# Marks up to sixteen ahead of each wait in a pair of tiles, and GpSimd's low parts after the counting

## What is computed

```python
xn = layernorm(x)
# graph part, twice: h = xn @ W.T + b; agg = segment_sum(h[src], dst); relu
# mixing part: q = softmax(xn @ Wq.T) * 512**-0.5; k = softmax(xn @ Wk.T, over nodes); v = xn @ Wv.T
#   y = q @ (k.T @ v) + xn;  y @ W1.T @ W2.T + y
x = x + graph + mixing
x = x + moe(layernorm(x))       # 8 experts, gates by 8 Sinkhorn rounds, top 156 rows each
```

## Time and profile before

| | us |
|---|---|
| median of 3 executions | 470.5 (470.48, 470.50, 472.29) |
| profiled execution, its own time | 470.02 |
| its span | 468.1 |
| PE busy in the span | 449.9 |
| DVE busy in the span | 333.2 |
| POOL busy in the span | 66.1 |

### The profile page before, as it was taken

How to read it: one execution, slowest core, us unless ns; L and a number is a source line. 1 busy time by engine, 2 the same in 40 slices (tenths; PEclk the granted TensorE clock), 3 DMA queues, 4 the chain that set the end, 5 groups by cost and what they waited for, 6 DMA issues and landing times.

```text
span 468.1 us, 7042 instructions
## 1 busy us (share of the span) xinstructions
PE 449.9 (96%) x2517; PEld 362.0 (77%) x2517; DVE 333.2 (71%) x1116; ACT 150.3 (32%) x274; POOL 66.1 (14%) x95
## 2 busy tenths in 40 slices
PE   8999999999999999899998999999999999888996
PEld 5877788889797979788787999877777775655783
DVE  5988599867868686888879960344545667777982
ACT  3666784223132323322240100223033124551120
POOL 5424700000000000000012000001400000006662
PEclk9999999999999999999999999999999999999999
DMA  8920200540000000203000000001844449405891
GB/s 250 265 78 2 90 0 1 137 97 11 1 1 0 2 1 8 85 0 127 1 5 2 2 0 1 1 0 20 296 131 133 133 135 366 170 1 169 295 366 73
DMA packets 20414, 40.46 MB, mean 86 GB/s; under 512 B 2521, under 2 KB 2851, under 8 KB 20373
## 3 DMA queue, kind: packets, MB, share of 16 engines
q1 hardware_dynamic: 18117, 32.53, 22.7%
q0 software_dynamic: 2256, 7.39, 4.5%
HBM read 30.09 MB, written 10.31 MB: 86 GB/s over the span
## 4 chain that ended last, share of the span: by engine, by line
PE 78%; DVE 13%; ACT 4%; issue 2%; DMA 1%; POOLq 0%; DVEq 0%; POOL 0%; SPq 0%
PE ps L769 29%; PE ps L1132 9%; PE ps L1024 9%; PE ps L952 6%; PE ps L897 6%; PE ps L756 4%; PE ps L970 2%; PE ps L811 2%; DVE RING_S L1877 2%; DVE RING_D L1876 2%; ACT scrap_a L1557 1%; DVE QTL L1811 1%; PE ps L1149 1%; ACT QTH L1287 1%; PE ps L945 1%
## 5 line engine op out<-in xcount | busy, mean ns | idle before, releaser
L1876 DVE TENSOR_SCALAR RING_D<-places,PLACES 125x170 bf16<-125x170 f16 x274 | 71.0, 259 | 3.2 <-issue 3.2
L1877 DVE TENSOR_SCALAR RING_S<-iota,HOME 125x128 bf16<-125x128 f16 x274 | 68.1, 249 | 0.0
L1024 PE MATMUL ps<-AT,H1H 125*128 125x416 f32 (+1 forms) x120 | 42.9, 358 | 0.3 <-ACT AT L1452 0.3
L1024 PE MATMUL ps<-AT,H1L 125*128 125x416 f32 (+1 forms) x120 | 42.2, 351 | 0.0
L756 PE MATMUL ps<-RING_D,RING_S 125*125 125x170 bf16 x274 | 35.2, 244 | 2.5 <-DVE RING_S L1877 0.9
L756 PEld LDWEIGHTS ps<-RING_D,RING_S 125*125 125x125 bf16 x274 | 27.5, 136 | 13.1 <-DVE RING_S L1877 7.1
L1132 PE MATMUL ps<-H2H,AT 125*125 125x512 f32 x90 | 36.1, 402 | 0.0
L1132 PE MATMUL ps<-H2L,AT 125*125 125x512 f32 x90 | 35.5, 394 | 0.0
L1149 PE MATMUL ps<-WE0H 128*128 128x512 f32 x129 | 35.5, 408 | 0.0
L630 POOL TENSOR_TENSOR G2L<-RAW_G,G2H 128x512 fp32r<-128x512 f32 x4 | 5.0, 1286 | 184.9 <-ACT G2H L1287 184.9
L1947 DVE TENSOR_TENSOR ps<-ps,bias 125x512 f32<-125x512 f32 x20 | 14.0, 699 | 20.4 <-PE ps L769 20.4
(11 more groups left out here) (413 smaller groups left out, 1156.5 us busy)
## 6 DMA issues: line engine op xcount, KB each, us to landing
RAW_E<-in_experts SPq DMA_DIRECT2D x8, 1024.0 KB, 9.9
RAW_AGAIN<-in_experts SPq DMA_DIRECT2D x3, 1024.0 KB, 9.5
X<-in_x SPq DMA_DIRECT2D x1, 2240.0 KB
out_x<-X SPq DMA_DIRECT2D x10, 224.0 KB
scratch<-X SPq DMA_DIRECT2D x10, 224.0 KB
scratch<-Y SPq DMA_DIRECT2D x10, 224.0 KB
RAW<-in_mW2T SPq DMA_DIRECT2D x4, 256.0 KB, 4.3
RAW_A<-in_mW SPq DMA_DIRECT2D x4, 256.0 KB, 4.7
```

The costliest lines, as they stand in the source:

```text
L1024: mm = pe.matmul(PS[plan[f"z{ch}_{f}"][0]][:, 0:c1 - c0], h[0:TT, k, 128 * f:128 * (f + 1)], AT[0:TT, k, c0:c1], start=(k == 0 and n == 0) ...
L1876: V.tensor_scalar(hot_d(v, width(b)), places[0:ET, 0:width(b)], PLACES[0:ET, c:c + 1], None, ALU.is_equal)
L1877: V.tensor_scalar(hot_s(v), iota[0:ET, :], HOME[0:ET, c:c + 1], None, ALU.is_equal).then_inc(done["marked"], 1)
```

## The change

The visits are laid a little differently: three instead of two at each of six places of the context, one fewer in `attend` of pairs 0 to 3 and in the second mix of pairs 1 to 3, one more in h2. In a pair DVE's steps get a new order. The eight matmuls with the identity of one `attend` become four of twice the columns, ahead of the wait for qtl_ready. Tile 9 is turned in the middle of the last mix of pair 3 (into another PSUM bank), and its low part stands ahead of that pair's last sum. Five marks go from behind the branch to ahead of it. POOL makes G2L only after all counts are stored.

```diff
--- before.py
+++ after.py
@@ -134,7 +134,7 @@
         for i in (2 * p, 2 * p + 1):
             use(f"xq{i}", (2, 3), ("mix_added", i + 1))
             if i + 2 < NT:
-                use(f"qt{i + 2}", (7,), ("qth_ready", i + 3), ("qtl_ready", i + 3))
+                use(f"qt{i + 2}", (7 if i + 2 < NT - 1 else 6,), ("qth_ready", i + 3), ("qtl_ready", i + 3))
     for i in range(NT):
         use(f"h{i}", (6, 7, 0, 1), ("h1h_ready", i + 1), ("h1l_ready", i + 1))
     for ch in range(3):
@@ -199,14 +199,14 @@
 def visits_in_products():
 
 
-    spots = [("cp", n, 2) for n in range(12, 48, 6)]
+    spots = [("cp", n, 3) for n in range(12, 48, 6)]
     for p in range(PAIRS):
         a, b = 2 * p + 2, 2 * p + 3
         if a < NT:
             spots += [(f"q{a}", 6, 7 if p else 5)]
-        spots += [(f"a{p}", 28, 8)]
+        spots += [(f"a{p}", 28, 7 if b < NT else 8)]
         if b < NT:
-            spots += [(f"q{b}", 6, 7), (f"x{a - 2}", 6, 7), (f"x{b - 2}", 6, 8)]
+            spots += [(f"q{b}", 6, 7), (f"x{a - 2}", 6, 7), (f"x{b - 2}", 6, 7 if p else 8)]
         else:
             spots += [(f"x{a - 2}", 0, 4), (f"x{a - 2}", 6, 5), (f"x{b - 2}", 6, 9)]
     for i in range(NT - 1):
@@ -666,6 +666,7 @@
                     link(ins)
             ins.then_inc(done["ranges"], 1)
 
+            pool.wait_ge(done["adj_hi"], NG)
             for c in range(C):
                 split_lo("g2", c)
 
@@ -937,12 +938,14 @@
                 for h in range(2):
                     ps = opens(f"at{p}_{h}")
                     visits(f"a{p}", 28 * h)
+                    both = ps[:, 0:4 * (TT + 1)].rearrange("p (k t n) -> p k t n", k=2, t=2)
+                    for n, x in enumerate((XTL, XTH)):
+                        pe.matmul(both, identr[:], x[:, 2 * p:2 * p + 2, 2 * h:2 * h + 2, 0:TT + 1].rearrange("p t k n -> p k t n"),
+                                  start=(n == 0), stop=False, skip_group_check=True)
                     for k in range(2):
                         f = 2 * h + k
                         block = slice(128 * f, 128 * (f + 1))
                         o = ps[:, 2 * (TT + 1) * k:2 * (TT + 1) * (k + 1)]
-                        for n, x in enumerate((XTH, XTL)):
-                            pe.matmul(o, identr[:], x[:, 2 * p:2 * p + 2, f, 0:TT + 1], start=(n == 0), stop=False, skip_group_check=True)
                         if f == 0:
                             pe.wait_ge(done["qtl_ready"], 2 * p + 2)
                             if p == 0:
@@ -952,11 +955,11 @@
                                 mm = pe.matmul(o, w[:, c, block], q[:, c].rearrange("p t n -> p (t n)"), start=False, stop=(c == C - 1 and n == 2), skip_group_check=True)
                     closes(f"at{p}_{h}", mm)
 
-            def mix(i):
+            def mix(i, **kw):
 
                 p, t = i // 2, i % 2
                 product(f"xq{i}", opens(f"xq{i}")[0:TT, :], (lambda c: SH[:, c, t, 0:TT], lambda c: SL[:, c, t, 0:TT]), (rows_of(MPH), rows_of(MPL)),
-                        before=lambda c: pe.wait_ge(done["sl_ready"], 2 * p + c // 2 + 1), unit=f"x{i}")
+                        before=lambda c: pe.wait_ge(done["sl_ready"], 2 * p + c // 2 + 1), unit=f"x{i}", **kw)
 
             pe.wait_ge(*lo_of("wv", C - 1))
             n = 0
@@ -980,9 +983,12 @@
                 if b < NT:
                     tile_product(f"q{b}", b, WQH, WQL, unit=f"q{b}")
                 for i in (2 * p, 2 * p + 1):
-                    mix(i)
-                    if i + 2 < NT:
-                        turn_q(i + 2)
+                    if i + 2 == NT - 1:
+                        mix(i, between=lambda: turn_q(NT - 1), at=7)
+                    else:
+                        mix(i)
+                        if i + 2 < NT:
+                            turn_q(i + 2)
             pe.wait_ge(*lo_of("g1", C - 1))
             for i in range(NT):
                 tile_product(f"h{i}", i, G1H, G1L, unit=f"h{i}")
@@ -1479,8 +1485,10 @@
                 if b < NT:
                     scale_q(b)
                     round_q(a)
+                if b == NT - 1:
+                    round_q(b)
                 groups_ending(f"x{b - 2}")
-                if b < NT:
+                if b < NT - 1:
                     round_q(b)
                 if b == NT - 1:
                     for c in range(C):
@@ -1907,39 +1915,43 @@
             context_left(3)
             for p in range(PAIRS):
                 a, b = 2 * p + 2, 2 * p + 3
-                mark_next(5)
+                mark_to(f"a{p}")
                 if a < NT:
                     q_peak(a)
+                    mark_next(3)
+                    q_inverse(a)
+                    mark_to(f"q{b}")
+                    attn_left(p, 0)
+                    mark_to(f"x{a - 2}")
+                    mark_next(2)
+                    attn_left(p, 1)
+                    mark_to(f"x{b - 2}")
+                    q_peak(b)
+                    mark_next(3)
+                    q_inverse(b)
+                    mark_to(f"q{a + 2}" if a + 2 < NT else f"a{p + 1}")
+                    add_mix(a - 2)
+                    q_left(a)
+                    if b < NT - 1:
+                        mark_next(3)
+                        add_mix(b - 2)
+                        q_left(b)
+                    else:
+                        q_left(b)
+                        mark_next(3)
+                        add_mix(b - 2)
                 else:
                     split_lo("g1", 0)
                     split_lo("g1", 1)
-                mark_to(f"a{p}")
-                if a < NT:
-                    q_inverse(a)
-                mark_next(3)
-                attn_left(p, 0)
-                if b < NT:
-                    mark_to(f"q{b}")
-                else:
+                    mark_to(f"x{a - 2}")
+                    attn_left(p, 0)
                     split_lo("g1", 2)
+                    attn_left(p, 1)
                     split_lo("g1", 3)
-                attn_left(p, 1)
-                if b < NT:
-                    mark_next(4)
-                    q_peak(b)
-                mark_to(f"x{a - 2}")
-                if b < NT:
-                    q_inverse(b)
-                mark_next(4)
-                add_mix(a - 2)
-                if b < NT:
-                    q_left(a)
-                mark_to(f"x{b - 2}")
-                mark_next(4)
-                add_mix(b - 2)
-                if b < NT:
-                    q_left(b)
-                mark_to(f"q{a + 2}" if a + 2 < NT else f"a{p + 1}" if b < NT else "h0")
+                    mark_to(f"x{b - 2}")
+                    add_mix(a - 2)
+                    mark_to("h0")
+                    add_mix(b - 2)
 
             def add_bias(layer, i):
                 ps = ps_of(f"h{i}" if layer == 1 else f"h2_{i}")[0:TT, :]
@@ -1961,6 +1973,7 @@
                 if i:
                     h1_left(i - 1)
             h1_left(NT - 1)
+            mark_next(5)
             dve.wait_ge(loads["pairs"], 32)
             after("flag_ready", 1)
             large = dve.value_load(flag[0:1, 0:1], min_val=0, max_val=1)
@@ -2044,7 +2057,7 @@
                 after("adj_hi", FIRST_LATE)
                 for u in range(2 * C):
                     ch, f = divmod(u, C)
-                    if u + 1 < 2 * C:
+                    if 0 < u < 2 * C - 1:
                         mark_next(5)
                     store_late(f"z{ch}_{f}")
                     if u + 1 < 2 * C:
```

## The result

The changed kernel takes 458.62 us (median of four runs, 457.58 to 460.1), the kernel before beside it 470.49 (470.29 to 472.29): a ratio of 0.974, 95% interval 0.970 to 0.978. The prediction said 460.0, and 458.0 to 464.2. The time lies in the range, and most terms of the sum behind it are right, but one step of it is wrong, and one thing that has nothing to do with the change hides that.

What follows compares the result with a forecast made beforehand. PE, busy 96% of the span, bounds the kernel; time is won where it waits for marks standing behind QTL in DVE's order. 7.2 + 1.3 + 0.7 + 1.3 = 10.5 off 470.5 gives 460.0 us, range 458.0 to 464.2.

Steps and rivals of the forecast that it cites:

- The heaps of the pairs (7.2): Pairs 0 to 3: DVE's new order makes marks ready before their visits, so all 7.2 us of PE's heap waits go.
- The last attend (1.3): Into the last pair: the earlier turn and QTL ahead of the sum remove attend's 1.3 us wait for QTL.
- Heap x9 (0.7): Heap x9: its nine marks follow G1L at once, so 0.7 us goes, the least certain heap, 0.3 to 0.7.
- Identity matmuls (nothing): Attend: eight identity matmuls become four of 504 columns, gaining nothing; bounds 0.5 us in all.
- POOL's wait (1.3): At the branch: POOL's G2L slows the first mark behind it; making POOL wait for all counts gains 1.3 us.
- The five marks moved ahead of the branch bring nothing: At the branch: DVE still makes nine marks, a copy and the pause in a row, so the gain is nothing.
- the 1.7 that was foretold: Heap z0_1 behind the branch: PE would still wait some 1.7 us there after the change.
- The chain to the end: Later stages: all follows on this chain, so the gain of 10.5 us goes through to the end.
- A: Pairs: a DVE step waits longer than allowed and one wait per pair stays, 4 x 1.0; 464.0 us, chance 0.13.
- B: Branch: DVE's pause goes with POOL's work, so 1.7 us more is won; 458.3 us, chance 0.07.
- C: Pairs: marks are not ahead, only G2L's 1.3 and the last attend's 1.3 come; 467.9 us, chance 0.05.
- D: Pairs: turning is late because tile b's reciprocal stands behind a waiting mark, making it slower; 475.2 us, chance 0.03.

Runs made afterwards that it cites:

- ten slots: The changed kernel with a ring of ten slots for marks instead of sixteen, nothing else: 465.34 us, one run.
- the second measurement: The changed kernel once more, with no edit, against the kernel before run beside it: 457.50 us, ratio 0.969 (0.966 to 0.972).
- five variants: Changed kernel with DVE's old order (465.92 us), ring of ten (465.34), without POOL's wait (460.32), seven marks ahead (457.85), marks before the copy (457.53).

## Why the prediction was right, and where not

- **The heaps of the pairs (7.2): right.** x4 and x5 fell from 0.92 and 1.79 to 0.69, q8 from 1.46 to 0.69, and the order by itself gave these 7.2 and x9's 0.7 (7.95 against 7.9). The order laid out by hand held: from q4's heap to q6's are 21.28, against 21.4 foretold.
- **The last attend (1.3): right in size, with more of a condition than was said.** The wait of 1.15 is gone from the changed kernel. The turn needs the new order to bring it; alone it brought 0.23, since DVE's work seems to bound that pair otherwise.
- **Heap x9 (0.7): right**, 1.53 to 0.84.
- **Identity matmuls (nothing): mis-sized.** They bring 0.42, inside the bound of 0.5; 0.23 of it is in the last attend's 1.3, where the prediction had it too. So the parts make 7.2 + 1.3 + 0.7 + 0.2 = 9.4 of the measured 9.74, and 0.3 is assigned to none; h0's first matmul came at 202.48, 200.6 without the late start, against 201.0.
- **POOL's wait (1.3): right.** Alone, 1.30. G2L at its new place held nothing up: ZL beside it, at 270.74 in the changed kernel, lasts 0.59, as elsewhere.
- **"The five marks moved ahead of the branch bring nothing": wrong.** They bring 1.6 to 1.7. The step put nine marks, a copy and the pause in a row; the pause isn't in that row, since it begins when the sequencer comes to the flag, with up to ten instructions passed on and not begun. The pause was marked "issue" in the earlier trace rows, and I didn't ask what DVE's queue held at that time. In before it held nothing behind the last H1L, so no mark lay beside the pause. For the same reason z0_1's heap waited 0.4 and not the 1.7 that was foretold.
- **The chain to the end: right.** From z0_1 on both kernels take 216.0; G2L at 268.94 ended 11 before z2 did, and no later stage grew.

Of the rivals, A (one wait a pair stays) didn't come; with ten slots it did, for 5.9, but at the turns. B foretold the time nearly (458.3) by a wrong mechanism: the pause doesn't depend on POOL, 3.24 with POOL away. C and D fell with the heaps at 0.69 and turns without a wait.

The forecast was 1.4 above the median of the first measurement and 2.5 above that of the second. Behind the first transpose 12.6 were won instead of 10.5: 1.6 by the marks, and 0.5 more in the pairs than the 9.2 of the sum. The base of 470.5 less 12.6 would have been 457.9. The four runs of the same program in the second measurement, 457.48 to 457.53, lie below the stated range; that the first measurement fell into it owes something to luck, at least in the profiled execution with its late start.

## What to carry to other kernels

An engine that makes what another eats should run its buffer's whole depth ahead, and steps with a late consumer go behind the makings, each where its own consumer still has time; a timeline laid out by hand from row durations is enough to find that order. At a branch or any other pause of a sequencer, count how many instructions its queue holds then (ten were passed on here): about that much work is free. Before moving VectorE work to a place, look whether GpSimd works there: two edits that are worth 1.3 and 0.3 alone were worth 2.97 together.

## What the runs showed of the hardware

**The granted clock can fall in the middle of the kernel.** Where PE waits long in the heap of z0_1 (2.9 to 3.4, beyond the 0.63 that nine ready visits take) it fell to 0.5, the 1.2 GHz level, for 3.4 us in three traces: DVE's order alone (245.07 to 248.48), the turn alone and the five marks alone. In the first of them PE had ended z0_0's product at full clock, began the heap at 241.99 and waited in it for marks; the fall came with the first matmuls of z0_1's product behind it. With waits of 3.1, 3.4 and 2.9 there, before, the identity merge alone and the changed kernel without POOL's wait show no fall, so such a wait doesn't always bring it. The windows of the kernel with DVE's order alone (length, then busy time of PE, PEld, DVE, ACT, POOL with counts, granted clock, DMA share, GB/s) and two of its matmuls, the second at full clock:

```profile
244.00:245.00 1.00, 0.73 (x3) 0.40 (x3) 1.00 (x7) 0.00 (x0) 0.00 (x0) 1.00 0.00 0
245.00:246.00 1.00, 0.95 (x4) 0.81 (x4) 1.00 (x5) 0.00 (x0) 0.00 (x0) 0.53 0.00 0
246.00:248.00 2.00, 2.00 (x8) 1.91 (x7) 2.00 (x11) 0.00 (x0) 0.00 (x0) 0.50 0.00 0
...
246.50 0.55 PE L1024 MATMUL ps<-AT,H1L 125*128 125x416 f32 x1
...
248.92 0.35 PE L1024 MATMUL ps<-AT,H1L 125*128 125x416 f32 x1
```

Matmuls then follow each other by 0.35 instead of 0.19, and z0_1 to h2 takes 45.4 to 45.5 instead of 43.9: 1.5 lost. The changed kernel waits 0.4 there, and its four runs in the second measurement lie 0.05 apart. The mean granted clock of each run tells more. Of 23 later runs of the kernel before, 17 have a mean of 0.991 to 0.996 and took 471.19 to 473.72; the other six, at 0.997 to 1.000, took 470.14 to 471.25 and once 472.43. The changed kernel's eight runs lie at 0.998 to 1.000. So part of what the second measurement gives the change (0.969 instead of 0.974) is very likely this fall, and taking the wait away also narrows the spread. Where in those runs the clock fell a mean doesn't say, and no profile of the kernel before with the fall was taken.

**The pause at the branch** is 3.24 of DVE standing still with POOL away. In the sequencer's own steps it is 3.76 to 3.95 from the load of the flag to the first step behind the branch, in all fourteen traces, and 2.79 to 2.97 of it lie behind the branch, whose own record lasts 0.07. In each of these traces a packet of 8 KB that the profile counts as "instruction", on queue 14, starts 0.8 to 1.0 after the branch and lands before the pause ends. The DMA view of before for 244.05 to 246.84, from the branch to the next step:

```profile
q14 instruction: 1, 0.01, 1.1%
```

This fits a sequencer that has to wait for the code of the other branch. No run varied it, so it isn't shown.

**The first stage** ended at 15.75 in one execution of the changed kernel and at 13.75 to 14.53 in the other and in its five variants; in the kernel before with DVE's order alone, whose code is the same up to there, it ended at 15.02. In the long one PE waited 1.35 for the first split weight. Its trace's record of the granted clock begins at 9.20, at the full level, in the other execution at 6.56; until about then matmuls of 512 columns follow each other by 0.47 instead of 0.23, so they ran at the lower level (1.2 GHz), though the view shows 1.00 from the start.
